# A state-space and attention kernel on one core: a new order of its front, and its last input rows made by other engines

## The reference, cut to what matters

```python
x_dbl = einsum('bld,ed->ble', x, x_proj_w)
dt, B_in, C_in = split(x_dbl, [128, 128 + 16], axis=-1)
delta = softplus(einsum('blr,dr->bld', dt, dt_proj_w) + dt_proj_b)
A = -exp(A_log)
def step(h, inp):                       # for each of the 1024 tokens
    dA = exp(dt_t[..., None] * A[None])
    dBx = dt_t[..., None] * B_t[:, None, :] * x_t[..., None]
    h = dA * h + dBx                    # 16 states for each channel
    y_t = einsum('bdn,bn->bd', h, C_t) + D_param * x_t
```

## Time and profile before

| | |
|---|---|
| median of three runs | 1816.66 us (1813.85 to 1820.73) |
| the profiled execution | 1827.84 us, of which its span 1826.1 us |
| TensorE busy | 1696.7 us, 93% of the span |
| VectorE, ScalarE, GpSimd busy | 1194.3, 1018.6, 778.9 us |
| mean granted TensorE clock | 0.976 |
| DMA, slices of 46 us from 0 | 148, 262, 221, 110, 97, 116, 273, 180 GB/s, then between 1 and 47 until 1370 us |

### The profile page before, as it was taken

The page is one execution under the profiler, slowest core; times in us unless marked ns, Lnnn a source line. Parts: engine busy times, 40 slices in busy tenths (PEclk is TensorE's granted clock), DMA queues, the critical chain, the costliest instruction groups (busy, mean ns, idle before and its releaser), DMA issues. The chain is left out here.

```text
span 1826.1 us, 33417 instructions
## 1 busy us (share of the span) xinstructions
PE 1696.7 (93%) x9234; PEld 1360.4 (74%) x9234; DVE 1194.3 (65%) x2422; ACT 1018.6 (56%) x2287; POOL 778.9 (43%) x789
## 2 busy tenths in 40 slices
PE   6399999489999999999999999999998999999997
PEld 2256556378888888888888888888885777666775
DVE  4799973597887766766767676667662344333476
ACT  4599943267665656665666566666652444434322
POOL 1489861453234544434443444344431342211463
PEclk9699999799999999999999999999999999999999
DMA  4653238500000100000000000001006999999433
GB/s 148 262 221 110 97 116 273 180 12 1 15 9 7 41 13 21 21 6 26 14 11 20 20 20 20 6 26 47 18 30 218 322 325 313 313 302 304 138 95 91
DMA packets 100395, 193.29 MB, mean 106 GB/s; under 512 B 15460, under 2 KB 59748, under 8 KB 97748
## 3 DMA queue, kind: packets, MB, share of 16 engines
q1 hardware_dynamic: 58836, 108.76, 19.1%
q0 software_dynamic: 17152, 47.67, 8.1%
q10 hardware_dynamic: 24336, 35.98, 5.9%
HBM read 140.84 MB, written 51.51 MB: 105 GB/s over the span
## 5 line engine op out<-in xcount | busy, mean ns | idle before, releaser
L1435 POOL TENSOR_TENSOR sw<-sw,rope_t 64x512 f32<-64x512 f32 x128 | 166.1, 1297 | 520.7 <-ACT sw L1048 495.1
L1077 ACT ACTIVATE pb<-ps,negmax 128x128 f32<-128x128 f32 (+7 forms) x256 | 190.8, 745 | 151.2 <-DVE negmax L1288 148.1
L963 PEld LDWEIGHTS ps<-pt,v 128*128 128x128 f32 x1280 | 242.1, 190 | 42.1 <-DVE xr L1316 4.0
L963 PE MATMUL ps<-pt,v 128*128 128x256 f32 (+1 forms) x1280 | 270.7, 358 | 2.8 <-DVE xr L1316 2.6
L561 POOL DMA_DIRECT2D w2r<-in_w x148 | 77.2, 522 | 320.1 <-PE ps L610 278.4
L644 DVE SCALAR_TENSOR_TENSOR ga<-th,ps 128x176 f32<-128x176 f32 x148 | 49.9, 337 | 230.0 <-ACT th L625 230.0
L1288 DVE TENSOR_REDUCE negmax<-ps 128x1 f32<-128x128 f32 (+7 forms) x256 | 193.9, 758 | 8.8
L1064 ACT COPY pt<-ps 128x512 f32<-128x512 f32 (+3 forms) x384 | 171.5, 484 | 38.7 <-PE ps L953 35.6
L1438 POOL TENSOR_TENSOR t<-t,sw 64x512 f32<-64x512 f32 x128 | 167.8, 1311 | 19.2 <-POOL sw L1435 12.8
L593 PE MATMUL ps<-w13r,xt 128*128 128x352 f32 x496 | 169.4, 464 | 0.0
L953 PE MATMUL ps<-ident,pb 128*128 128x128 f32 x1152 | 167.5, 272 | 0.0
(11 more groups left out here) (245 smaller groups left out, 4004.6 us busy)
## 6 DMA issues: line engine op xcount, KB each, us to landing
w13r<-in_w SPq DMA_DIRECT2D x124, 352.0 KB, 5.5
w2r<-in_w POOLq DMA_DIRECT2D x148, 176.0 KB, 5.8
result<-yy ACTq DMA_DIRECT2D x148, 128.0 KB, 4.9
crow<-c_rows SPq DMA_DIRECT2D x32, 512.0 KB, 3.5
t<-sorted SPq DMA_DIRECT2D x124, 128.0 KB, 5.1
sorted<-zeros ACTq DMA_DIRECT2D x15, 1024.0 KB, 16.9
hc<-in_w SPq DMA_DIRECT2D x24, 352.0 KB, 5.1
wraw<-in_wqk SPq DMA_DIRECT2D x16, 256.0 KB
```

The costliest lines, as they stand in the source:

```text
L963: last = pe.matmul(ps[:, 6, c0:2 * P], v[:, j, hd], pt[g % 2][:, j, c0:2 * P], start=j == 0, stop=j == 2 * g + 1)
L1077: act.activation(pb[:, qt % 2, 0:cols], ps[:, bank:bank + 2, :].rearrange("p a n -> p (a n)")[:, 0:cols], ACT.Exp, bias=negmax[:, par, qn: ...
L1435: g.tensor_tensor(sw[64:128, p % 2, :], sw[64:128, p % 2, :], rope_t[64:128, 1, (p // 2) * 512:(p // 2 + 1) * 512], ALU.mult).then_inc(s_t ...
```

## The change

Five edits in one:

- TensorE, ScalarE and VectorE take the front in another order: the dt rows of groups 0 and 1 first, then softplus pieces 0 and 1 (the first batch), with the B/C rows and the dt rows of groups 2 and 3 between them. The routing stands behind the second piece instead of ahead of the first. TensorE makes pieces 2 and 3 before the routing's matmuls instead of after them.
- The input rows of batch 0 stand behind piece 2 on VectorE and those of batch 1 behind piece 3, so pieces 2 and 3 are no longer next to each other.
- `last_block` leaves VectorE. For q = 0 GpSimd makes it, one pair ahead, behind the first product of a pair; for q = 1 ScalarE makes it as an eighth block. The spread waits for GpSimd's block before its first transpose instead of before its eighth.
- ScalarE's first two decays wait for three and four deltas instead of both for four.
- The second zero fill leaves ScalarE. SyncE issues it in the attention, 31 DMAs of 512 KB out of a new zero tile that VectorE clears before the attention, between the first turn of the loop of loads and the rest. The waits for it on VectorE and ScalarE ahead of the attention are gone.

The diff, cut to its core:

```diff
+        R1.zero_dmas = R1.routed * P // 512
+        zero_tile = sbo("zero_tile", [P, 4 * D])
@@ att_sp
-            with sp.Fori(0, PAIRS_H - 1) as hp:
+            def load_pair(hp):
                 load_qk(2 * hp + 2)
                 load_qk(2 * hp + 3)
                 load_values(hp + 1)
                 load_wo(2 * hp + 2)
                 load_wo(2 * hp + 3)
+            load_pair(0)
+            sp.wait_ge(s_kept, 1)
+            for k in range(R1.zero_dmas):
+                sp.dma_start(R1.slots[k * 512:(k + 1) * 512, :].rearrange("(p a) d -> p (a d)", p=P), zero_tile[:]).then_inc(R1.zeroed, 16)
+            with sp.Fori(1, PAIRS_H - 1) as hp:
+                load_pair(hp)
@@ gpsimd
+            def last_block(b, j):
+                if not isinstance(j, int) or j > 0:
+                    g.wait_ge(s_dbx, 4 * j - 2)
+                g.tensor_tensor(dbxT[:, 0, TB - 1, :], dxT[:, b * TB + TB - 1, :],
+                                b_col[:, b * TB + TB - 1, bass.ds(2 * j - b * STATES, 1)].to_broadcast([P, D]), ALU.mult).then_inc(s_dbxL, 1)
             def weigh(b, j, next_b):
...
                         g.tensor_tensor(hc[:, q, c], state[:, q, c], crow[:, q], ALU.mult).then_inc(s_hc, 1)
+                        if q == 0 and c == 0 and next_b < BATCH:
+                            last_block(next_b, j + 1)
+            g.wait_ge(s_col, 1)
+            g.wait_ge(s_dxT, TB // 2)
+            last_block(0, 0)
@@ vector
+            softplus(0)
+            take_bc_rows(0)
+            take_bc_rows(1)
+            softplus(1, last_bc_rows)       # rows 2 and 3 ahead of its fourth step
             v.wait_ge(R0.logits_ready, 1)
...
             route_dve(v, R0)
+            softplus(2)
+            input_rows(0)
+            softplus(3)
+            input_rows(1)
...
-            def last_block(b, it, q):
-                w(v, s_dbx, 2 * it - 2)
-                v.tensor_scalar(dbxT[:, q, TB - 1, :], dxT[:, b * TB + TB - 1, :], b_col[:, b * TB + TB - 1, bass.ds(it - b * STATES, 1)],
-                                None, ALU.mult).then_inc(s_dbxL, 1)
+            def scans(j):
                 for q in range(2):
+                    for c in range(DC):
+                        scan(2 * j + q, q, c)
...
-            v.wait_ge(R1.zeroed, 16 * R1.zero_dmas)
+            v.memset(zero_tile[:], 0.0).then_inc(s_kept, 1)
@@ scalar
+            take_group(0)
+            take_group(1)
+            take_dt_rows(0)
+            take_group(2)
+            take_dt_rows(1)
+            take_group(3)
+            act.wait_ge(s_const, N_CONST + 4)
+            softplus(0)
+            take_dt_rows(2)
+            take_dt_rows(3)
+            for p in range(1, BATCH * DC):
+                softplus(p)
-            zero_fill(act, R1)
...
-                    for i in range(TB - 1):
+                    for i in range(TB - 1 + q):
...
-                    if isinstance(it, int) and it == 0:
-                        act.wait_ge(s_delta, BATCH * DC)
+                    if isinstance(it, int) and it < 2:
+                        act.wait_ge(s_delta, 3 + it)
...
-            act.wait_ge(R1.zeroed, 16 * R1.zero_dmas)
@@ tensor
             def dt_piece(p):
                 b, c = p // DC, p % DC
+                pe.wait_ge(s_xdc, 2 * b + 2)
                 if p >= 2:
                     pe.wait_ge(s_dpc, 2 * p - 2)
+                else:
+                    pe.wait_ge(s_xnT, p + 3)
...
+            turn_group(0)
+            turn_group(1)
+            pe.wait_ge(s_par, 80)
+            dt_rows(0)
+            turn_group(2)
+            dt_rows(1)
+            turn_group(3)
+            for p in range(2):
+                dt_piece(p)
+            bc_rows(0)
+            bc_rows(1)
+            dt_rows(2)
+            dt_rows(3)
+            for p in range(2, BATCH * DC):
+                dt_piece(p)
+            bc_rows(2)
+            bc_rows(3)
+            pe.wait_ge(s_bcc, NG)
...
+            def spread(j, q, c):
+                it = 2 * j + q
                 if c == 0:
                     pe.wait_ge(s_dbxT, it + 1)
+                    if q == 0:
+                        pe.wait_ge(s_dbxL, j + 1)
                 if not (isinstance(it, int) and it == 0):
                     pe.wait_ge(s_scan, 2 * it + c - 1)
                 for i in range(TB):
-                    if c == 0 and i == TB - 1:
-                        pe.wait_ge(s_dbxL, it + 1)
```

More of the change, by code:

```diff
@@ L1803, in _, with take_group, take_dt_rows, softplus @@
             act.mul(aneg[:], alog[:], -1.0).then_inc(s_aneg, 1)
[L1805 to L1815 removed]
+            def take_group(q):
+                act.wait_ge(s_xnT_ps, q + 1)
+                for c in range(DC):
+                    last = act.copy(xnT[:, c, q * 512:(q + 1) * 512], ps[:, (q % 2) * 2 + c, :])
+                last.then_inc(s_xnT, 1)
+            def take_dt_rows(g):
+                act.wait_ge(s_xd, g + 1)
+                act.copy(dtT[:, g * 512:(g + 1) * 512], ps[:, 4 + g % 2, :]).then_inc(s_xdc, 1)
+            def softplus(p):
                 c = p % DC
@@ new lines, in turn_group, with dt_rows @@
+            def turn_group(q):
+                pe.wait_ge(s_xn, q + 1)
+                if q >= 2:
+                    pe.wait_ge(s_xnT, q - 1)
+                for c in range(DC):
+                    for i in range(GT):
+                        last = pe.transpose(ps[:, (q % 2) * 2 + c, i * P:(i + 1) * P], xn[:, q * GT + i, c * P:(c + 1) * P], ident[:])
+                last.then_inc(s_xnT_ps, 1)
+            def dt_rows(g):
+                pe.wait_ge(s_xnT, g + 1)
+                if g >= 2:
+                    pe.wait_ge(s_xdc, g - 1)
+                for c in range(DC):
+                    last = pe.matmul(ps[:, 4 + g % 2, :], xpw[:, c, 0:RANK], xnT[:, c, g * 512:(g + 1) * 512],
+                                     start=c == 0, stop=c == DC - 1)
+                last.then_inc(s_xd, 1)
@@ L1914, in dt_piece, with bc_rows @@
+            def bc_rows(g):
+                pe.wait_ge(s_xnT, g + 1)
+                if g >= 2:
+                    pe.wait_ge(s_bcc, g - 1)
+                for c in range(DC):
+                    last = pe.matmul(ps[0:BCR, 6 + g % 2, :], xpw[:, c, RANK:XD], xnT[:, c, g * 512:(g + 1) * 512],
+                                     start=c == 0, stop=c == DC - 1)
+                last.then_inc(s_xb, 1)
             def dt_piece(p):
                 b, c = p // DC, p % DC
+                pe.wait_ge(s_xdc, 2 * b + 2)
@@ L1943, in delta_rows @@
                     last.then_inc(s_dlT, 1)
+            turn_group(0)
[16 more added lines that the diff above has]
+            pe.wait_ge(s_bcc, NG)
+            for i in range(NT):
+                last = pe.transpose(ps[:, 4 + i // 8, (i % 8) * BCR:(i % 8 + 1) * BCR], bcT[:, i * P:(i + 1) * P], ident[0:BCR, 0:BCR])
+            last.then_inc(R0.logits_ready, 1)
+            route_pe(pe, R0)
             pe.wait_ge(R0.slots_ready, 1)
@@ L1972, in _ @@
                         for c in range(DC):
-                            spread(it, q, c)
+                            spread(j, q, c)
                             if it >= 2:
```

116 lines of the change are left out of this document (32 added, 84 removed).

## The result

On the chip of the first measurement the changed kernel takes 1795.3 us (median of 4 runs, 1793.08 to 1807.11) beside 1818.7 for the kernel before (4 runs, 1813.85 to 1822.07): ratio 0.9887, 95% interval 0.9859 to 0.9915, so 20.6 us less (15.5 to 25.6); the medians alone are 23.4 apart. Forecast were 1807.0, range 1802.5 to 1813.0, and a gain of 9.7. On two other chips the same pair gave 0.9895 (0.9868 to 0.9921) and 0.9920 (0.9899 to 0.9942).

A forecast was written before the change was run, and what follows sets the result against it. TensorE was taken to bound the state stage, its start held by ScalarE behind the second fill. Start 8.0 + run-up 0.8 + gaps 0.88 and 0.4 - lag 0.4 = 9.7 us: 1816.66 to 1807.0, range 1802.5 to 1813.0.

The forecast's parts named there:

- Start: Start of the state stage: TensorE's first transposes of the input term at 80.4 instead of 88.39, 8.0 us earlier.
- The forecast's own lower bound: First transposes at 78.4 if GpSimd's 16 scatters take 20.9 us at the undisturbed pitch.
- Run-up: From first transposes to the third state's: 8.85 us instead of 9.65, paced by VectorE's scans, gain 0.8.
- Gap at the C row: State stage: the half step made too long by a C row behind the fill becomes normal, 0.88 us back.
- long last blocks: State stage: VectorE's long last blocks cost one more half step 0.4 us, which comes back.
- lag of GpSimd: State loop: 0.4 us taken off the gain, half of GpSimd's possible lag with the added block.
- the unseen block: GpSimd's 128x256 product with a broadcast column, not in the trace: priced at 0.75 us.
- it moves as a whole: Everything after the state stage is issued by work and TensorE-bound, so the same 9.7 us come off the whole time.
- GpSimd is the bound: Rival, state loop: at 1.3 us a block GpSimd lags 0.49 a pair, net gain 3.6, time 1813; chance 0.15.
- Blocked scatters: Rival, front: scatters wait for VectorE's softplus steps and take 27 us, TensorE starts at 84.5, time 1811; chance 0.12.
- The fill collides in the attention: Rival: fill below 206 GB/s delays GpSimd's scatter; at 180 GB/s it ends 20 us late, time 1827; chance 0.04.
- More than forecast: Rival, front: scatters at the plain pitch throughout, start 78.5, time 1805 or 1804; chance 0.09.

The follow-up runs named there:

- e9: The changed kernel's text unedited, run again on the chip of e8 to e11: 0.9920 of the kernel before, -14.7 us.
- e5: The changed kernel's text unedited, run again on the chip of e5 to e7: 0.9895 of the kernel before, -19.1 us.
- e13: The changed kernel unedited, one profiled execution on one further chip: state stage ends at 251.0 us, first expert stage takes 318.7.
- e15: The changed kernel unedited, a second single execution on the chip of e13: state stage ends at 250.7 us, first expert stage takes 333.9.
- e6: The kernel before, unedited, compared with itself: ratio 0.9998, -0.4 us.
- e12: The kernel before unedited, one profiled execution on the chip of e13: state stage ends at 264.1 us, first expert stage takes 325.3.
- e14: The kernel before unedited, a second single execution on the chip of e13: state stage ends at 264.3 us, first expert stage takes 326.6.
- M: Part of the change: second zero fill moved from ScalarE to SyncE in the attention. Alone on the kernel before (e1): 0.9964, -6.6 us.
- e1: The kernel before with only the second zero fill moved from ScalarE to SyncE's attention loads: 0.9964, -6.6 us.
- e4: The changed kernel with all last blocks put back on VectorE; new front and moved fill stay: 0.9924 of before, -13.9 us.
- e7: The kernel before with the fill moved to SyncE and last blocks on GpSimd and ScalarE, front order old: 0.9917, -15.1 us.
- e8: The changed kernel with the second fill issued by SyncE at the very front instead of in the attention: 0.9913 of before, -16.0 us.
- e2: The kernel before with only the new front order; fill by ScalarE, last blocks by VectorE: 0.9946, -9.9 us.
- e3: The changed kernel with only the second fill put back on ScalarE, behind the last softplus piece: 0.9967 of before, -6.0 us.
- e10: The text of e3 run again, on the chip of e8 to e11: 0.9948 of before, -9.5 us.
- e11: The kernel before with only the last blocks moved to GpSimd and ScalarE: 1.0010, +1.8 us.
- B: Part of the change: last blocks moved from VectorE to GpSimd and ScalarE. Alone on the kernel before (e11): 1.0010, +1.8 us.

## Why the forecast was right in kind and wrong in size

**The state stage: 12.9 us, forecast 9.7.** Mean of the ends over four executions of before (262.7, 263.6, 264.1, 264.3) 263.7, over five of after (249.3, 253.4, 249.4, 251.0, 250.7) 250.8. By the terms of the sum:

- Start, forecast 8.0: measured 10.7 in the first profiles, 10.6 in the means (89.0 to 78.4). This is the term of the sum that was mis-sized. Its parts: the columns came at 44.65, where 46.1 was laid out, 1.45 (VectorE's second softplus pass began at 37.26, where my summed front had 38.3); the scatters took 21.9 instead of 22.9, since two of them were long (2.06 and 1.55) where the earlier trace rows made me expect nearly three, 1.0; the block 0.617 and its hand-over, 0.2 to 0.3. The forecast's own lower bound for this step, 78.4, is the mean that was measured; its value, 80.4, was not reached in any of five executions.
- Run-up, forecast 0.8: 1.34 between the first profiles, 0.9 between the means. In all four executions of before it is 9.65 or 9.66, in after 8.31 and 8.36 (e9) or 8.99 (e5, e13, e15). What differs is TensorE's granted clock. In after it is 1.00, the level of 2.4 GHz, from 76 to 78 us, and the first 16 transposes take 2.97 (above); in e13 it is 0.50, the level of 1.2 GHz, from 60 to 86 us:

```profile
78.66 3.65 PE L2006 MATMUL ps<-ident,dbxT 128*128 128x128 f32 x16 [2.82 <-POOL dbxT L1607]
```

  The 2.0 that I laid out up to the first scan came from the earlier trace rows, where the clock was the low one; with the high one it was 1.40 (77.66 to 79.06). e5, whose state stage ends latest of the five, stayed at 0.50 up to about 92, and its third state's first half step took 4.35 in place of 2.6. Why the clock rose at different times stays open.
- Gap at the C row 0.88, long last blocks 0.4, lag of GpSimd -0.4: the stage behind the run-up is 155.65 - 154.31 = 1.34 shorter, against 0.88 after the lag. Of the other executions of before, e6 has a gap of 0.56 at the late C row and e12 and e14 have none there, but 2.1 in the third state's first half step at granted 0.50. GpSimd never held TensorE in the loop, so the lag of 0.4 was not there. It had been put in for the price of the unseen block: bounds 0.40 and 0.931, taken 0.75, found 0.617. On VectorE an undisturbed block took 0.33, one beside GpSimd's product up to 2.55. The Trainium skill, page "GPSIMD Engine Reference", has GpSimd about twice slower in work with two inputs (section Engine selection). 0.617 against 0.33 is 1.9, but VectorE's block is a TENSOR_SCALAR with one tensor as input, so this is no like-for-like test. The estimate of 0.56 from the slope in its section on elementwise cost was nearer to the measured 0.617 than my line through two rows (0.72, taken as 0.75).

**What follows: "it moves as a whole" is the step that took the time out of the range.** It failed as a statement on single executions, and may have failed on the kernel. The 3.2 us by which the state stage was mis-sized would have left the time inside the range: 1816.66 - 12.9 = 1803.8, or 1805.8 from 1818.7. The attention does move as a whole (984.1 to 984.6 in every execution of either kernel). Behind it the expert stage of layer 1 runs with its DMA engines full and takes 313 to 334 us. The page of after, DMA share in tenths and GB/s over 40 slices of 44.8 us; the stage fills slices 32 to 37, counted from 1, at 313 to 324 GB/s:

```profile
DMA  3232339400090100000000000001004999999633
GB/s 127 81 107 94 105 109 309 144 7 1 16 371 11 39 13 22 21 6 26 15 12 20 19 7 29 12 20 38 28 25 151 320 324 313 315 323 322 196 112 100
```

The three timed comparisons give 20.6, 19.1 and 14.7, mean 18.1, each within 4 to 5 either way, and the state stage accounts for 12.9. By the end of the attention the means of the profiles are 14.1 apart (1369.5 and 1355.4); the 1.2 more lie in the stretch of layer 0's experts, which takes 118.7 to 120.9 in after and 120.3 to 123.6 in before. Some 4 us more are measured and not explained.

They lean towards M. Set beside each kernel's own profile at the end of the attention (1369.5 less that end), the seven comparisons with the fill away from ScalarE gain 5.4, 8.3 and -0.2 (after, e5, e9), 4.0, 8.2, 7.5 and 5.6 (e1, e4, e7, e8) more than the profile shows; those with it there -2.1, -0.7, 4.7 and 0.6 (e2, e3, e10, e11). On the chip of e8 to e11 the leaning is reversed between e9 and e10. The mean of the profiled expert stage is 319.8 in nine executions of the first kind and 323.4 in eight of the second. With a spread of 20 us within one kernel, and one profile for most kernels, that is a leaning, not a finding. Whether M makes that stage a little faster stays open.

**The rivals.** *GpSimd is the bound*: no, 4 x 2.366 + 0.617 = 10.08 a pair against 10.37. *Blocked scatters*: no, 21.9 in place of 27. Two of 16 were long, by 1.09 and 0.58 over the plain 0.97, again at the beginning of a softplus pass; beside the other eight steps of VectorE they took 0.96 to 1.03. The Trainium skill, page "SBUF — State Buffer", section on the two separate sides, lets a VectorE step with two SBUF inputs and a GpSimd operation that reads SBUF block each other for the whole instruction. If a scatter is such an operation, these rows show it for two of ten steps at most. *The fill collides in the attention*: not with after. *More than forecast* was the right one in kind, given 0.09, but my price for it (1804 to 1805) stopped at the bounds of the start and left nothing for a later stage. The range did that too: it was built from the terms of the front with 2 us for the medians, while the runs of before already went from 1813.85 to 1820.73 and the profiled one stood 11.2 above their median. That distance was a warning that executions differ somewhere; a second profiled execution of before would have shown where (the tail, below).

## To carry to other kernels

Price a moved step by what stands behind it in its queue: the block on GpSimd is free with the C row on time and costs TensorE 3.75 us when it is late, so M had to come with B. Then ask of a change in several parts what each is worth on top of the others: here one part, the front's order, brings 12.1 of the 12.9 us of the state stage, and M and B together add 0.8 to it. Before a difference of two profiled executions is read, put the stage borders of several executions of each kernel side by side: here 13 of 33 us were shown to be the change, 14 lay in a stretch whose length goes with the chip (below), and one stage of one kernel alone varied by 20. Where a bound in the forecast comes from the plain pitch and the value from a few disturbed rows, keep the range open on the plain side.

## What the runs showed of the hardware

**ScalarE standing in a loop with no releaser.** e1 and e4 lose 4 to 6 us in the attention (988.4 and 989.9 instead of 984.1 to 984.6). The fill's transfer is not the cause: the first loss stands at 760 us, over 200 behind its end in e1. ScalarE's timeline in e1 there, then at the same place of the loop in after:

```profile
757.23 0.19 ACT L1079 ACTIVATION_READ_ACCUMULATOR pb<-ps,negmax 128x1 f32 x1
759.85 0.27 ACT L1066 COPY pt<-ps 128x128 f32<-128x128 f32 x1 [2.43 <-issue]
760.01 0.62 ACT L1085 CAST qkr<-t 128x512 fp32r<-128x512 f32 x1
761.90 0.58 ACT L1049 COPY sw<-ps 32x512 f32<-32x512 f32 x1 [1.27 <-issue]
```

```profile
749.01 0.19 ACT L1079 ACTIVATION_READ_ACCUMULATOR pb<-ps,negmax 128x1 f32 x1
749.18 0.27 ACT L1066 COPY pt<-ps 128x128 f32<-128x128 f32 x1
749.59 0.62 ACT L1085 CAST qkr<-t 128x512 fp32r<-128x512 f32 x1
751.01 0.58 ACT L1049 COPY sw<-ps 32x512 f32<-32x512 f32 x1 [0.79 <-PE ps L887]
```

In e1 ScalarE stands twice with nothing that the profile shows to wait for, and the page's instruction queue q14 moved more there than in after (packets, MB, share), first e1, then after:

```profile
q14 instruction: 56, 0.45, 0.1%
```

```profile
q14 instruction: 36, 0.29, 0.1%
```

e4 has 55 packets, the other fifteen profiled executions have 36 or 37. The first of the two waits comes four times in each of them, 124 us apart, at 2.1 to 2.4, and each time TensorE stands 1.0 to 1.5 a few us later. What e1 and e4 share and the others lack is a ScalarE program without the fill and with VectorE's last blocks, that is the shortest one. That its loop then lies worse for the loading of instructions, so that ScalarE waits for its own, is my reading; no run moved the loop alone.

**A tail of 110 or 125 us.** The shared experts at the end take 110.2 to 110.9 us in eight executions and 124.0 to 126.9 in nine, of both kernels, and of one text (after: e5 and e9) once so and once so. In the fifteen executions of the experiments the length goes with the chip and not with the kernel: 126.5 to 126.9 in e1 to e4 and 125.5 to 126.6 in e8 to e11, 110.2 to 110.9 in e5 to e7 and 110.2 to 110.6 in e12 to e15, each group on a chip of its own. The timed medians of before agree: 1831.8 and 1834.3 us on the two chips with the long tail, 1816.1 and 1818.7 on the chip of e5 to e7 and on that of the first measurement, where the tail of after is short. What differs between the chips stays open. In the short executions ScalarE waits for VectorE; in the long ones a large part of that has no releaser. ScalarE's waits behind the last gate-up, in e5, then in e9 (waiter, released by: us in total, times, longest):

```profile
ACT sh_hr L774 <- DVE sh_h L811: 55.7, 24, 3.8
ACT sh_th L769 <- PE ps L887: 10.3, 10, 2.4
```

```profile
ACT sh_hr L774 <- DVE sh_h L811: 27.4, 14, 3.9
ACT sh_hr L774 <- issue: 21.0, 9, 3.8
```

Neither the clock (0.97 granted in the long one of before, 0.98 in the short one of after) nor the DMA engines (share 0.30 and 0.34) tell them apart. The profiled execution of before was a long one and that of after a short one, and 13.7 us of their difference are just this. At 1827.84 it also lies above every timed run of before on the chip of the first measurement (1822.07 at most), as if it came from another chip; that is not shown. A ratio taken on one chip is free of this.
